# Moving the second attention's sum, transposes, projection and residual, its exponential, and a bias addition in a two-layer transformer kernel

## The reference

```python
x = x + attn0(layernorm(x)) + ffn0(layernorm(x))          # layer 0
xn = layernorm(x)
# layer 1, attention: 16 heads of 8, for every one of the 512 positions over the 8 batch entries
q, k, v = xn @ Wq.T + bq, xn @ Wk.T + bk, xn @ Wv.T + bv
p = softmax(einsum('nqd,nkd->nqk', q, k) * HD ** -0.5)    # 8 x 8 scores for each position and head
a = einsum('nqk,nkd->nqd', p, v) @ out_w.T + out_b
# layer 1, mixture of experts: 16 experts of width 64, 4 chosen by grouped top-k, and a shared one
g = silu(einsum('th,efh->tef', xn, w1_e)); u = einsum('th,efh->tef', xn, w3_e)
routed = einsum('tef,ehf,te->th', g * u, w2_e, combine)
shared = (silu(xn @ w1_s.T) * (xn @ w3_s.T)) @ w2_s.T
x = x + a + routed + shared
```

## Time and profile before

| | us |
|---|---|
| median of 3 runs | 361.5 (361.3 to 362.45) |
| the profiled execution, as timed | 361.89 |
| its span, first to last instruction | 360.1 |
| TensorE busy | 306.7 (85%) |
| VectorE busy | 314.0 (87%) |
| ScalarE busy | 178.7 (50%) |
| GpSimd busy | 250.5 (70%) |

### The profile page before, as it was taken

One profiled execution on the slowest core, in us unless ns is written; L12 is line 12 of the kernel. 1 busy time (PEld: TensorE's weight loads), 2 busy tenths in 40 slices (PEclk: granted clock), 3 DMA queues, 4 the chain that ended last, 5 costly groups with the idle time before them and its releaser, 6 DMA issues. The chain is left out here.

```text
span 360.1 us, 5666 instructions
## 1 busy us (share of the span) xinstructions
PE 306.7 (85%) x1771; PEld 252.2 (70%) x1771; DVE 314.0 (87%) x826; ACT 178.7 (50%) x499; POOL 250.5 (70%) x162
## 2 busy tenths in 40 slices
PE   0568876889898887588989999999989989999895
PEld 0346665767686666477868887887879878798675
DVE  5995899989878777976999999899998999989795
ACT  3345755878777667676241623425325253252520
POOL 4184577836657482214989889879898798987771
PEclk9987999999999999979999999999999999999999
DMA  5690000000000000004953424313443334253201
GB/s 139 168 295 1 2 0 1 2 2 0 3 0 3 0 0 3 0 5 121 175 130 98 110 83 104 101 63 121 116 96 100 109 106 99 69 136 97 49 2 58
DMA packets 21321, 24.91 MB, mean 69 GB/s; under 512 B 2420, under 2 KB 12060, under 8 KB 21292
## 3 DMA queue, kind: packets, MB, share of 16 engines
q1 hardware_dynamic: 20248, 24.09, 25.4%
q10 hardware_dynamic: 820, 0.39, 0.4%
q0 software_dynamic: 224, 0.08, 0.1%
HBM read 22.19 MB, written 2.36 MB: 68 GB/s over the span
## 5 line engine op out<-in xcount | busy, mean ns | idle before, releaser
L885 POOL TENSOR_TENSOR prod_pv<-prob,qkv 128x1024 f32<-128x1024 f32 x32 | 69.6, 2196 | 16.9 <-DVE att L1589 15.1
L875 POOL TENSOR_TENSOR prod_qk<-qkv 128x1024 f32<-128x1024 f32 x32 | 76.7, 2413 | 4.6 <-DVE above L1459 4.6
L773 ACT ACTIVATE Q<-Q 128x512 f32<-128x512 f32 x48 | 27.3, 582 | 47.2 <-PE Q L942 47.2
L942 PE MATMUL Q<-bias,ones 128*128 128x400 f32 (+1 forms) x64 | 30.7, 480 | 15.9 <-ACT v_ext L663 7.0
L1575 DVE TENSOR_REDUCE scr<-prod_qk 128x128 f32<-128x1024 f32 x32 | 38.8, 1213 | 5.4 <-POOL prod_qk L875 5.4
L1630 DVE TENSOR_TENSOR hid<-T,sgc 128x512 f32<-128x512 f32 x64 | 43.4, 677 | 0.1
L942 PEld LDWEIGHTS Q<-w,hid 128*128 128x128 f32 x288 | 37.5, 191 | 3.6 <-DVE hid L1630 0.7
L942 PEld LDWEIGHTS VN<-w,hid 128*128 128x128 f32 x288 | 37.7, 191 | 3.0
L942 PE MATMUL Q<-w,hid 128*128 128x128 f32 x288 | 38.0, 275 | 0.5 <-DVE hid L1630 0.5
L1589 DVE TENSOR_REDUCE att<-prod_pv 128x128 f32<-128x1024 f32 x32 | 38.2, 1194 | 0.0
L942 PE MATMUL VN<-w,hid 128*128 128x128 f32 x288 | 37.9, 274 | 0.0
(11 more groups left out here) (186 smaller groups left out, 809.5 us busy)
## 6 DMA issues: line engine op xcount, KB each, us to landing
cw<-comb_table SPq DMA_DIRECT2D x62, 256.0 KB, 4.7
out_x<-fin SPq DMA_DIRECT2D x7, 256.0 KB, 4.6
x<-in_x SPq DMA_DIRECT2D x2, 256.0 KB, 3.0
wraw<-in_w1T SPq DMA_DIRECT2D x1, 512.0 KB, 4.0
w3raw<-in_w3T SPq DMA_DIRECT2D x1, 512.0 KB, 4.7
w<-in_w2T SPq DMA_DIRECT2D x1, 512.0 KB, 5.7
cw<-comb_table SPq DMA_DIRECT2D x4, 128.0 KB, 3.4
rope_s<-in_c_sin ACTq DMA_DIRECT2D x1, 256.0 KB, 5.0
```

What stands on the lines that cost most here:

```text
L773: act.activation(gated[:, :], gate_bank(n, s)[:, :], ACT.Silu).then_inc(sg_ready, 1)
L875: pool.tensor_tensor(prod_qk[:, t % 2], bc(qkv2[:, TH * half + t, j, 0:D], 1, NB), qkv2[:, :, j, D:2 * D], ALU.mult).then_inc(qk_prod, 1)
L885: pool.tensor_tensor(prod_pv[:, t % 2].rearrange("p (h e) b -> p b h e", e=HD), bc(prob[:, t].rearrange("p h b -> p b h"), 3, HD), qkv2[:, ...
L942: return pe.matmul(o, lhsT, rhs, start=start, stop=stop)
```

## The change

Everything is in the second part, but for the bias.

- Slots 0 to 6: `exp_done` at step 2 instead of 1, that is behind one more Silu. `attention_transposes` and `attT_evac` at step 9 instead of 8, `attention_product` at 12 instead of 11. `sum_of_p` at step 5 instead of 2, `over_sum` at 6 instead of 3. `residual` at 14 instead of 13 (slot 6 stays at 15).
- Slot 7 keeps all its steps.
- `biased`: out of the first part's steps. Entries 0 and 1 come in front of the first `product_qk`, entries 2 to 7 each between product_qk(n+1, 0) and less_max(n) of slots n = 0 to 5. `residual` waits only for the entries of its half.

```diff
@@ ScalarE
                 for u, p in units(k):
-                    if p == 1:
+                    if p == (1 if u == END else 2):
                         exp_done(u)
-                    if p == 8:
+                    if p == (8 if u == END else 9):
                         attT_evac(u)
@@ GpSimd
-                run(i, 5, biased)
                 run(i, 1, mx_over_scale)
...
+            biased(0)
+            biased(1)
             pool.wait_ge(l1_kept, NT)
             pool.wait_ge(r_step, R_ABOVE)
             for t in range(TH):
                 product_qk(0, t, 0, 0)
-            biased(NB - 1)
...
                 next_qk(0)
+                if n + 2 < NB:
+                    biased(n + 2)
                 less_max(n)
                 next_qk(1)
@@ TensorE
-                    if p == (9 if u == END else 11):
+                    if p == (9 if u == END else 12):
                         attention_product(u)
-                    if p == 8:
+                    if p == (8 if u == END else 9):
...
                         attention_transposes(u)
@@ VectorE
-                dve.wait_ge(x_biased, NB)
+                dve.wait_ge(x_biased, TH * half + TH)
...
-                if p == 2:
+                if p == (2 if u == END else 5):
                     sum_of_p(u)
-                if p == 3:
+                if p == (3 if u == END else 6):
                     over_sum(u)
...
-                if p == (10 if u == END else 15 if u == END - 1 else 13):
+                if p == (10 if u == END else 15 if u == END - 1 else 14):
                     residual(u)
```

## The result

| | before | after |
|---|---|---|
| median of 6 runs, us | 361.4 (360.65 to 362.45) | 355.25 (354.41 to 355.92) |
| the profiled execution, as timed | 361.89 | 355.92 |
| its span | 360.1 | 354.1 |
| first part, to the `pairs` of VectorE that waits 4.26 us for ScalarE | 164.27 | 161.77 |
| second part, from there to VectorE's end | 193.34 | 189.86 |

The ratio is 0.9828, with a 95% interval of 0.9807 to 0.9849. The change gains 6.15 us, where 3.6 were forecast and the range ended at a gain of 4.7. The split tells where the rest came from. The second part gained 3.48 us, which is the forecast. The first part, in which the change only takes out the bias additions, gained 2.5 us, where I had written "nothing".

A forecast was written before the change was run, and what follows sets the result against it. VectorE sets the pace, so only its idle time can go: 0.62 + 0.3 + 0.2 + 0.55 + 1.65 + 0.47 = 3.8 us, taken as 3.6. Profiled execution 358.3, median 357.9 us, range 356.8 to 360.5.

The forecast's parts named there:

- The change, part by part: Costing of each move; its first term put removing eight 1.27 us bias additions from the first part at nothing.
- The first part as long as before: Sign that the forecast is right: the first part keeps its length, though the bias additions leave it.
- The weighed rule: Skill's rule: two-SBUF-input VectorE operations and SBUF-reading GpSimd ones exclude each other; at most some 6 us, nothing added.
- (a): VectorE's sgc at step 2 waits for the Silu behind the Exp, slots 1, 3, 5; gains 0.62, 0.3, 0.2 us.
- (c): Second scr of the next slot waits for prod_qk in slots 2, 4, 6; 1.23 us in one, to stay unchanged.
- (d): Third scr waits for prod_qk behind four prod_pv, slots 4 and 6, trace in 2; 1.65 us to go.
- (e): sgc waits for a Silu behind the copy of the transposes, 0.25 us and a trace in slot 6; 0.47 gained.
- (b): Slot 7: sgc at step 2 waits 2.48 us for the Silu behind the Exp; gain 0.55, leaving 1.9 to 2.0.
- The rival in which GpSimd becomes the bound: Second part: late products leave four bias additions in the loop, 5.1 us lost against 4.0 won, 362.6; chance 0.08.
- The held Exp: Rival, slots 3 and 5: later transposes make the step 3 wait 1.7 us; 1.5 gained, 360.0; chance 0.14.
- the trade of places: Rival: time freed by (d) returns at the next slot's second scr, 361 us; chance 0.11.
- The residual a slice later: Slots 0 to 2: first down of slot n+2 waits 0.3 to 0.5 us on TensorE, covered; cost nothing.

The follow-up runs named there:

- e2: Kernel after the change, with the bias additions back in the first part as before: 357.8 us, ratio 0.9897.
- e1: Kernel before the change, with only the bias additions moved as in the change: 362.06 us, ratio 1.0009.
- e7: Kernel after the change, with the Exp back at step 1 in all slots: 360.03 us, ratio 0.9951.
- e9: Kernel after, with transposes and copy of slots 2 and 4 back at step 8 and w3's low part moved from step 4 to 9: 353.47 us.
- e5: Kernel after the change, with a spare GpSimd memset of 1400 elements a partition in the bias addition's old place: 357.93 us, ratio 0.9891.
- e11: Kernel after the change, with a spare GpSimd addition over 512 elements in the bias addition's old place: 356.55 us, ratio 0.9856.

## Why the prediction was wrong, point by point

**The step that failed** is the first term of "The change, part by part": "In the first part they filled idle time [...] I cost their removal at nothing." That GpSimd was idle there is true. But the argument asks only whether GpSimd had time, and not what its work does to other engines. The removal was worth five times about 0.54 us: 15.62 - 15.08 a step, 2.5 to 2.7 us in all. That is the whole miss, since 6.15 - 3.6 is 2.55. With it, the sum of the prediction comes to 361.89 - 3.6 - 2.6 = 355.7 for the profiled execution, which took 355.92. "The first part as long as before", among what would show it right, was wrong, and no rival spoke of the first part at all. The row that carries it was there to be seen: a group of twelve like instructions with a median of 170 ns and a longest of 772.

**The weighed rule**, on two SBUF inputs, gave no reason for a cost in the second part, and there was none: with bias additions beside `hid`, `sgc` and `fin`, e2 and after have the same 189.86 us. What I did not weigh was another rule for another place, `TENSOR_SCALAR` in the first part.

**Kinds of waits in the second part**, forecast and measured:

| | before | forecast | after |
|---|---|---|---|
| (a) `sgc` at step 2, slots 1, 3, 5 | 0.54, 1.11, 1.06 | none | none |
| slot 3: at step 3, and second `scr` | 1.11 | 0.8 to 0.9, as one | 0.59 and 0.22 |
| slot 5: second `scr`, `sgc` | 1.06 | 0.75 and 0.2 | 0.69 and 0.13 |
| (c) second `scr`, slots 2, 4, 6 | 1.08, 1.23, 1.22 | unchanged | 1.08, 1.21, 1.21 |
| (d) third `scr`, slots 4, 6 | 0.68, 0.67 | none | none |
| (e) `sgc` behind the copy, slot 4 | 0.25 | none | none |
| (b) slot 7 | 2.48 | 1.9 to 2.0 | 1.82 |

The rows of after for (c) in slot 2, for the second `scr` in slot 5 and for slot 7:

```profile
226.40 1.22 DVE L1577 TENSOR_REDUCE scr<-prod_qk 128x128 f32<-128x1024 f32 x1 [1.08 <-POOL prod_qk L874]
293.29 1.22 DVE L1577 TENSOR_REDUCE scr<-prod_qk 128x128 f32<-128x1024 f32 x1 [0.69 <-POOL prod_qk L874]
335.72 0.69 DVE L1619 TENSOR_TENSOR sgc<-VN,cw 128x512 f32<-128x512 f32 x1 [1.82 <-ACT VN L773]
```

The wait in slot 3 was put down to one place and stood in two. The bias addition ahead of `less_max` there makes `prod_qk` late as well, which I had seen for slot 5 only. The sum was near: 0.81. The 0.13 of slot 5 is read from two rows, as `sgc` starts at 295.23 and `hid` ahead of it ends at 295.11.

The wait forecast for `prod_qk` in slot 5, 0.75, was met by 0.69, but its working does not add up. From one `less_max` to the next stand eight products, not nine, and the parts that are listed come to 25.6 us and not to 22.1. The trace of after has 22.26 us from the `less_max` at 267.57 to the one at 289.83, with 0.83 of waits for `att`.

**The Exp** ends 4.2 us after the row maximum in slots 3 and 5 and 2.4 in slots 2, 4 and 6, against "4.2 in the worst slots, and 2 to 3 elsewhere". In slot 3 the maximum ends at 244.46 + 0.68 = 245.14 and the Exp at 248.73 + 0.63 = 249.36.

**GpSimd.** The products wait 2.9 us for `att` (below 7 was forecast). `less_max` waits 2.7 us for `smax` over the six slots of the stretch (below 3 was forecast, 4.2 before). The rival in which GpSimd becomes the bound did not come about in after, but it is real. e1 is that case: the bias additions in the loop without the room that the later sum makes. There the products still wait 12.0 us for `att`, and the second part is 3.1 us longer, where the rival had 5.1.

**The held Exp and the trade of places** did not come about. In after, the waits that went did not come back elsewhere. What I had not seen is how near the held Exp was: e7 shows 4.3 us for leaving one line out.

**The residual a slice later** was costed at nothing. The waits of VectorE that the table lists fall by 3.37 us, and two waits fewer give 0.16 more, so that the 3.48 us measured leave no room for a cost there; but it was not tried alone, and that it costs nothing is argued and not shown.

## What to carry to other kernels

Before work is moved to or from GpSimd, look for VectorE instructions of one group whose longest is several times their median, and see whether they end with a GpSimd operation; an idle GpSimd says nothing of what its work costs VectorE's chain. A held instruction is not yet a cost: `root<-mv` over 8 elements is held in every kernel here, up to 1.22 us in after, and in the steps from 70 us on `root<-ss` behind it waits for ScalarE in any case (0.47 us at 71.20). Whether the other held ones cost anything was tried only for the one that e9 frees. The remedy is often only to exchange two GpSimd instructions, so that the movable one runs while VectorE does reductions or reads PSUM. And where an engine runs its queue in order, moves of two instructions that end up side by side are one change, to be costed together.

## What the runs showed of the hardware

- A VectorE `TENSOR_SCALAR` of 8 to 16 elements a partition with input and output in SBUF, 0.16 to 0.17 us when free, ended 0.02 to 0.05 us after a GpSimd operation that ran beside it, wherever it took longer: 0.53 us under an addition of 1.05 us, 0.77 under one of 1.27, and 1.57 under the low part of 3.02.
- A memset on GpSimd, which reads nothing, held it as well: 0.73 us in place of 0.17, at 117.38 in e5.
- In e5, three held instructions stayed so through the change from `rope_ab` to the memset: `root<-mv` took 1.85 us from 69.42 to 71.27, and 1.86 in the next two steps. Where the bias addition (before) or the spare addition (e11) followed `rope_ab` it ended with `rope_ab`, at 0.66 us. Why the memset differs is open.
- Reductions were not seen held: `amax<-xn` took 0.68 us in e5, begun at 70.63 under the memset, and 0.68 in after with no GpSimd operation beside it. The 32 reductions `scr<-prod_qk` of after, over 1024 elements, took 1.20 to 1.22 us each, in a part in which GpSimd is busy 168.85 of 192.3 us.
